# A decoder layer with a mixture of experts: another order of each engine's work within an expert, other PSUM banks for the last two chunks, and the experts' output tiles evicted by ScalarE

## The reference, cut to what matters

```python
def _mlp(h, wg, wu, wd):
    return jax.nn.silu(h @ wg) * (h @ wu) @ wd
C = int(np.ceil(1.25 * N * 2 / 16))          # 640 rows for each expert, N = 4096
expert_inputs = jnp.zeros((E, C, d)).at[idx_flat, pos_c].add(x_pair)   # gathered tokens
expert_outputs = jax.vmap(_mlp)(expert_inputs, w_gate, w_up, w_down)   # F = 704
output_tokens = (expert_outputs[idx_flat, pos_c] * (vals_flat * within)[:, None])...
return x + _mlp(x, sw_gate, sw_up, sw_down) + output_tokens
```

## Time and profile before

| what | value |
|---|---|
| median of 3 runs | 1927.52 us (1926.8 to 1929.26) |
| profiled execution, its own time | 1925.47 us |
| its span, first to last instruction | 1923.8 us |
| TensorE busy (matmuls) | 1810.9 us, 94% |
| VectorE, ScalarE, GpSimd busy | 1243.3, 889.0, 1054.0 us |
| mean granted TensorE clock | 0.971 |

### The profile page before, as it was taken

How to read it: one execution, slowest core, us unless ns; L and a number is a source line. 1 busy time by engine, 2 the same in 40 slices (tenths; PEclk the granted TensorE clock), 3 DMA queues, 4 the chain that set the end, 5 groups by cost and what they waited for, 6 DMA issues and landing times.

```text
span 1923.8 us, 27307 instructions
## 1 busy us (share of the span) xinstructions
PE 1810.9 (94%) x9689; PEld 1595.2 (83%) x9689; DVE 1243.3 (65%) x2579; ACT 889.0 (46%) x1638; POOL 1054.0 (55%) x809
## 2 busy tenths in 40 slices
PE   9999999999999999999998998899889988998897
PEld 6888888888878888888888888888788888888887
DVE  6677777778644444437675777567666766686663
ACT  5465556564643333315454445344534553554341
POOL 3444546556442222246657755775577557755861
PEclk9999999999999999999999999999999999999999
DMA  9354555443423332245547555654575456546642
GB/s 330 117 143 130 133 144 148 147 140 103 116 37 44 45 78 45 44 101 132 103 133 165 122 100 140 156 125 101 135 160 118 106 142 151 114 115 146 145 86 28
DMA packets 236007, 229.35 MB, mean 119 GB/s; under 512 B 169664, under 2 KB 169920, under 8 KB 234592
## 3 DMA queue, kind: packets, MB, share of 16 engines
q1 hardware_dynamic: 210432, 174.50, 33.4%
q0 software_dynamic: 25440, 53.11, 15.7%
HBM read 138.80 MB, written 49.97 MB: 98 GB/s over the span
## 4 chain that ended last, share of the span: by engine, by line
PE 50%; DVE 16%; POOL 14%; issue 9%; ACT 6%; DMA 4%; POOLq 0%; SPq 0%; DVEq 0%; ACTq 0%
PE ps L73 31%; PE ps L2111 8%; PE ps L2140 7%; POOL out_tokens L1570 6%; POOL buffer L1528 5%; ACT buffer L1618 4%; PE ps L1003 3%; DMA buffer<-in_wts 3%; DVE buffer L1804 2%; DVE ps L1855 2%; POOL buffer L1533 1%; DVE buffer L1812 1%; DVE buffer L1936 1%; ACT buffer L1670 1%; PE ps L1147 1%
## 5 line engine op out<-in xcount | busy, mean ns | idle before, releaser
L73 PE MATMUL ps<-buffer,buffer 128*128 128x512 f32 (+1 forms) x4596 | 912.1, 357 | 33.1 <-DVE buffer L1913 32.4
L73 PEld LDWEIGHTS ps<-buffer,buffer 128*128 128x128 f32 x4596 | 785.9, 188 | 143.6 <-DVE buffer L1913 36.6
L1618 ACT ACTIVATE buffer<-buffer 128x512 fp32r<-128x512 f32 (+7 forms) x555 | 379.5, 736 | 245.2 <-DMA buffer<-in_wts 148.3
L2140 PE MATMUL ps<-buffer,buffer 128*128 128x512 f32 (+1 forms) x1921 | 439.1, 389 | 3.1 <-DVE buffer L1848 3.1
L2140 PEld LDWEIGHTS ps<-buffer,buffer 128*128 128x128 f32 x1921 | 357.9, 188 | 77.1 <-issue 3.7
L2111 PE MATMUL ps<-buffer,buffer 128*128 128x320 f32 x2016 | 341.6, 333 | 64.5 <-ACT buffer L1618 63.3
L2111 PEld LDWEIGHTS ps<-buffer,buffer 128*128 128x128 f32 x2016 | 332.4, 209 | 69.8 <-ACT buffer L1618 67.3
L1528 POOL TENSOR_TENSOR buffer<-buffer,buffer 128x512 fp32r<-128x512 f32 x176 | 260.3, 1729 | 26.2 <-ACT buffer L1618 26.2
L1533 POOL TENSOR_TENSOR buffer<-buffer,buffer 128x768 fp32r<-128x768 f32 x48 | 89.6, 1866 | 237.8 <-ACT buffer L1618 237.3
L521 POOL DMA_INDIRECT slots<-pairs,slot_u x64 | 63.5, 992 | 209.1 <-DVE slot_u L990 192.0
L1570 POOL DMA_INDIRECT out_tokens<-buffer,slot_list x79 | 130.0, 1645 | 55.7 <-DVE buffer L1936 32.5
(11 more groups left out here) (162 smaller groups left out, 1865.8 us busy)
## 6 DMA issues: line engine op xcount, KB each, us to landing
buffer<-in_wts SPq DMA_DIRECT2D x128, 512.0 KB, 3.7
buffer<-in_wts SPq DMA_DIRECT2D x33, 256.0 KB, 3.5
buffer<-in_xT SPq DMA_DIRECT2D x8, 1024.0 KB, 5.5
buffer<-in_ctxT SPq DMA_DIRECT2D x8, 1024.0 KB, 8.0
out_tokens<-buffer SPq DMA_DIRECT2D x8, 1024.0 KB, 4.3
tokens_normed<-buffer SPq DMA_DIRECT2D x32, 256.0 KB, 2.9
out_tokens<-buffer POOLq DMA_DIRECT2D x32, 256.0 KB, 6.7
buffer<-in_x SPq DMA_DIRECT2D x7, 1024.0 KB, 5.7
```

The lines of the kernel that those rows point to most:

```text
L73: last = pe.matmul(out, left, right, start=(c == 0 and i == 0), stop=(c == len(parts) - 1 and i == 2))
L1618: return act.activation(dst, src, ACT.Copy)
L2140: ins = pe.matmul(down_bank[(n + i) % 2][:, part_cols], left, right, start=(c == 0 and k == 0), stop=(c == FC - 1 and k == len(passes) - 1))
```

## The change

No instruction's work is changed in the attention blocks or the shared expert; the order of some of SyncE's loads and transposes for expert 0 is. In the expert loop:

1. The order of each engine's calls is written out anew, in whole blocks, and the counts that its waits use come from lists of names in that order (`numbered`) in place of formulas. `pair_high` is cut into `block_high` and `sum_high`, `pair_low` into `block_low` and `sum_low`, the second add of `third` becomes `up_b`, and each x_top, x_hi, x_sum_hi, gather, turn, scatter and evict can stand by itself. TensorE's own order stays the same.
2. The units of chunk 4 (half A) and chunk 5 (half A) take the two down banks; paired chunks 1 and 3 always take `even_banks`, chunk 2 `odd_banks`; 0A even, 0B and 4B odd, 5B the bank ps[1]. The product is written over the gate's bank in place of a third one. Waits follow (`bank_free`).
3. The experts' output tiles are evicted by ScalarE, as a copy with the routing weight as scale, in place of VectorE's multiplication.
4. `third_sum` has two buffers that take turns; some buffers move in SBUF to make room.

The core of the diff:

```diff
-    banks = [(ps[0], ps[1], ps[2]), (ps[3], ps[6], ps[7])]
+    even_banks, odd_banks = (ps[0], ps[1], ps[2]), (ps[3], ps[6], ps[7])
+    pair_banks = {1: even_banks, 2: odd_banks, 3: even_banks}
...
+    def plain_banks(e, c, j):
+
+        a = tiles_before[B + e] % 2
+        if c == FC - 1:
+            return [(down_bank[1 - a], down_bank[1 - a]), (ps[1], ps[1])][j]
+        if (c, j) == (4, 0):
+            return down_bank[a], down_bank[1 - a]
+        return (even_banks, odd_banks)[j][0:2]
...
+            elif what == "m36":
+                low_ready(pe, e, 1, 0)
...
+            elif what == "4A":
+                pe.wait_ge(s_ost, tiles_before[B + e])
+            elif what == "4B":
+                pair_silu_ready(pe, e, "a", 2)
+                low_ready(pe, e, 2, 0)
+            elif what == "5A":
+                product_ready(pe, e, 4, 0)
+            elif what == "5B":
+                low_ready(pe, e, 3, 0)
...
+        def evict(e, t):
+            g = B + e
+            n = tiles_before[g] + t
+            act.wait_ge(s_add[t], 16 * adds_of(g, t))
...
+            gate = slot_list[:, e * ET + t, 1:2]
+            for i, cols in enumerate(column_parts(g, t)):
+                act.wait_ge(s_down, n + i + 1)
+                act.activation(ost[:, t, cols], down_bank[(n + i) % 2][:, cols], ACT.Copy, scale=gate).then_inc(s_ost, 1)
```

More of the change, by code:

```diff
@@ L1269, in phase2, with numbered @@
[L1269 to L1281, removed]
+    def numbered(first, steady):
+        number = {}
+        for name in first.split():
+            number[name, 0] = len(number) + 1
+        for e in range(E):
+            for name in steady.split():
+                of = e + name.endswith("+")
+                if of < E:
+                    number[name.rstrip("+"), of] = len(number) + 1
+        return number
@@ L1283, in pair_no, with pair_before @@
     def pair_no(e, c):
         return NP * e + PAIRED.index(c)
[L1286 to L1290, removed]
+    def pair_before(e, c, k):
+        n = pair_no(e, c) - k
+        return n // NP, PAIRED[n % NP]
+    def plain_banks(e, c, j):
[5 more added lines that the diff above has]
+        return (even_banks, odd_banks)[j][0:2]
@@ L1300, in product_count @@
[L1300 to L1308, removed]
     FIRST = WC - 1
@@ L1583, in gpsimd @@
                 pool.wait_ge(s_list, 16)
-                gather(0)
+                for t in range(ET):
+                    gather(0, t)
             for c in range(FC):
@@ L1757, in scalar @@
             plain_hi(e, 0, 1)
-            for i in range(8, NPL):
-                plain_high(e, i)
+            plain_high(e, 10)
             paired_silu_a(e, 1)
@@ L1789, in scalar @@
             if more:
-                tokens(e + 1)
-                pair_high(e + 1, 2)
-                for i in range(2, 5):
-                    plain_high(e + 1, i)
+                x_top(e + 1, 0)
+                x_top(e + 1, 1)
+                sum_high(e + 1, 2)
+                x_top(e + 1, 2)
+            evict(e, 0)
+            if more:
+                plain_high(e + 1, 2)
+                plain_high(e + 1, 3)
+                x_top(e + 1, 3)
+                x_top(e + 1, 4)
+                x_hi(e + 1, 0)
+            evict(e, 1)
+            if more:
+                x_hi(e + 1, 1)
+                plain_high(e + 1, 4)
+            evict(e, 2)
+            if more:
+                x_sum_hi(e + 1, 0)
+                x_sum_hi(e + 1, 2)
+                x_sum_hi(e + 1, 1)
+                x_sum_hi(e + 1, 3)
+            evict(e, 3)
+            evict(e, 4)
     def vector(dve):
@@ L1915, in evict @@
         def evict(g, t):
-            job, part, _, _ = groups[g]
             n = tiles_before[g] + t
@@ L2006, in vector @@
             paired_product(e, 1, 0)
+            if more:
+                pair_sums(e + 1, 0)
+            paired_lo(e, 1, 0)
+            third(e, 2)
             paired_product(e, 1, 1)
-            paired_lo(e, 1, 0)
+            up_b(e, 2)
+            second(e, 3)
             paired_lo(e, 1, 1)
-            third(e, 2)
-            second(e, 3)
             up_a(e, 2)
@@ L2123, in down @@
                     pe.wait_ge(s_ost, n - 1)
+                if g >= B and t < 2:
+                    bank_free(g - B, f"d{t}")
                 cols = slice(t * P, (t + 1) * P)
```

633 lines of the change are left out of this document (357 added, 276 removed).

## The result

The changed kernel takes 1881.53 us in the median of 4 runs (1878.29 to 1884.4), against 1927.52: a ratio of 0.976, 95% interval 0.9743 to 0.9777. That is 46 us less, where 124 were forecast, and it lies outside the range of 1786 to 1855. The profiled execution's span is 1876.5 us.

What follows compares the result with a forecast made beforehand. TensorE, busy 94%, was taken as the bound, so only its idle time and clock could give. Expert 0 ends at 943.95; 14 x 56.5 = 791.0 and 65.6 lead to 1800.6; plus 1.7 and 2.0: 1804 us, range 1786 to 1855.

Steps and rivals of the forecast that it cites:

- The long wait and its clock: In each expert, ahead of product 2.2: the 4.26 us wait and the 2.88 us of slow clock both go.
- Weight sums ahead of 1A's low part: Ahead of product 3.6: VectorE's sums make TensorE wait 0.8 us, plus 0.2 for the queue, 1.0 for each expert.
- Wait in 4B: 4B no longer needs 3A's low part, so 1.99 us goes; 5B's bank was to be early by 1.7 us.
- rival A: GpSimd's scatters held beside VectorE's token splits; 3.6 us wait ahead of product 3.6, not 0.8; 1843 us, chance 0.13.
- Rival C: TensorE's clock falls all the same after 1 us idles, costing 2.9 us each expert; 1847 us, chance 0.05.
- Evictions: Five for each expert on ScalarE, 0.65 us each: cost 0 in the down product, with 1.3 to 1.6 us cover.
- Expert 0: Shared down's tile 2 waits 1.5 us, first units 1.8 more; it ends at 943.95 against 943.77, nothing won.
- The end: The last stretch, 72.92 us, loses its wait (3.98), clock (2.9) and 0.4: 65.6 us, to 1800.6.
- the hand schedule: TensorE's parts of one expert laid out at full clock, 55.5 us, plus 1.0 of waiting: 56.5 for each expert.

Runs made afterwards that it cites:

- The one move in the kernel before: Kernel before, with ScalarE making the high part of chunk 3's next block ahead of 5A's silu, its sums' ahead of the tokens' copies: 1906.94 us, 0.989.
- the runs above: The best kernel with 4B's second bank waiting for 3A's low part, 1832.81 us; the changed kernel with weight sums moved ahead of chunk 3's adds, 1864.92 us.
- products in PSUM: Changed kernel with the B halves' silu and product written into the gate's PSUM bank: 1814.89 us, 0.9415.
- the two edits: Changed kernel with B halves' silu and product in PSUM, and all gathers ahead of the low parts of blocks 0 and 1: 1800.17 us, 0.9338.
- one bank dependence: 4B's second bank again waits for the low part of 3A: 1937.63 us in the changed kernel, 1832.81 us in the best kernel.
- the evictions' place: Experts' evictions back on VectorE among the token work: 1887.49 us in the changed kernel, 1813.78 us in the best kernel.
- the bank wait in the best kernel: The best kernel with 4B's second bank waiting for the low part of 3A again: 1832.81 us, 0.952.
- the best kernel: Changed kernel with both B halves' products in PSUM and all gathers ahead of the low parts of blocks 0 and 1: 1800.17 us, 0.9338.

## Why the prediction was wrong

**The long wait and its clock: right.** GpSimd's scatters start 4.8 us before an expert ends (1068.21 against 1073.00), where 5.3 were forecast; load 8 goes out at 7.4 of the next expert (5.5 forecast), `first` of chunk 2 ends at 12.9 and TensorE needs it at 15.8. The one move in the kernel before confirms the chain.

**The step that failed first: "Weight sums ahead of 1A's low part", 1.0 us for an expert.** It measured 2.5 and 1.6 of clock behind it, 3.1 of the 5.0 us that an expert took too long. The four sums took 4.3 us, from 16.0 to 20.4; the prediction had the start right to the tenth and bounded them by 3.4, with the longest duration of the row of before (2.26), where VectorE met one GpSimd subtraction. Here it met two in a row and was held over both. The bound was not one. Load 1 went out at 12.4, not 10.5, so its 2 us of slack were gone too, but VectorE's waits for it are 0.3 us at most.

**The second step that failed: "Wait in 4B", put at nothing.** The 1.99 goes, but 1.4 came back ahead of 5B, and 0.5 in down. The prediction took the 3.7 us from product 3.3 to the low part of 3A from the trace of before. It was 6.7 here (1044.62 to 1051.28), because VectorE's whole queue was late by the 4.35 us low part of 1B, by a sum of 2.10 and by a product of 2.27, all held. The prediction set the two queues side by side only at the sums and, in rival A, at the scatters, and did not ask what else would now run at once. Counted by cause, that missing term is the larger error: with the low part and product of the B halves no longer held, the period is 57.15, near the 56.5 forecast, since GpSimd then also meets the sums a microsecond earlier and the clock stays whole.

**Clock.** The prediction gave the wait ahead of 3.6 no clock, because 1.8 us of idle had left it whole. The kernel before spoke for that more strongly than the earlier trace rows show: of its 15 waits of 1.8 to 2.5 us in 4B, 14 left it at 1.00. In the changed kernel all 14 waits of 2.3 to 2.7 us ahead of 3.6 were followed by half clock. So the length of an idle does not settle it, here or in the runs above where 1.9 us lowered it and 2.65 did not; what does is open. Rival C named this effect, for idles of 1 us in each expert; the idles of 1.2 to 1.5 us here and with products in PSUM left the clock whole.

**Evictions: near right.** They take 0.69 us (0.65 forecast), eviction 0 ends at 49.4 after down's start at 41.7: tile 2 begins at 50.0. Down waits for no eviction, with 0.5 us to spare where 1.6 were forecast. Their worth was put at nothing and is 14 us once nothing else binds.

**Expert 0.** Forecast to start at 885.65 and end at 943.95; it was 888.02 and 949.95. Down waited 2.55 for the eviction where 1.5 was forecast, and half clock lay behind it. **The end:** 65.0 against 65.6.

By the prediction's sum: 6.0 for expert 0, 14 x 5.0 = 70.6 for the periods and -0.6 for the end lead from 1800.6 to 1876.6; the span is 1876.5. Where VectorE is not held on TensorE's chains, the whole work takes 1800 us. That is near the 1804 forecast in part by luck: its periods are 55.67 where 56.5 were forecast, 12 us less, and its expert 0 ends 9.5 us later than forecast. The periods still say that the hand schedule was right for a VectorE that GpSimd does not stop.

**The rule that was on the table.** The trace: in the places read here, two-buffer operations of VectorE end when GpSimd's run of subtractions ends, 3.2 us in place of 0.4, 4.4 and 7.7 in place of 0.5; those that read PSUM and one buffer kept 0.48 beside them. The Trainium skill says it in SBUF — State Buffer, SBUF: two separate sides: the shared pair of ports is an exclusive lock for a whole instruction, also between a VectorE operation with two SBUF inputs and a GpSimd operation that reads SBUF. The trace agrees and goes further, since one VectorE operation was held over four GpSimd instructions. The kernel before showed holds too, at the low parts of the token sums, 1.9 us in the median in place of 0.82. Rival A named the rule, and put it at the scatters in place of the sums and products. That section of the Trainium skill tells of starved descriptor writing for another mode of VectorE's operations, its two-port mode, so that A's use of it went beyond what is written there; here the first three scatters, beside VectorE's two-buffer operations, took 1.9 to 2.6 us in place of 1.55, and no wait of TensorE stands on them.

## What to carry to other kernels

Before moving an operation, list for its new place which VectorE operations with two SBUF inputs and which GpSimd operations will run side by side, and give each of the first the length of the whole run of the second as its upper bound. Where such an operation stands in a chain that TensorE waits for, keep one of its inputs in PSUM, or put DMA issues rather than subtractions beside it: the two edits took 81 us off the changed kernel. A busy time that rises while work is taken away is the sign to look for, and a part's worth depends on the others: one bank dependence cost 56 or 33 us, the evictions' place 6, hardly measurable, or 14.

## What the runs showed of the hardware that was not expected

- A VectorE operation of 0.48 us was held for 7.68, through four GpSimd subtractions that followed each other without a gap, and had been issued 0.6 us ahead of the first of them, at the end of a gather. GpSimd's gathers alone did not hold it: four sums at 0.42 to 0.43 us beside two gathers.
- Not every meeting lasts a whole run. In the kernel before, three low parts of the token sums took 4.93 us (0.82 each alone) beside three subtractions that took 5.55 (1.3 each alone, in the changed kernel): the two engines went in turn, and each held the other. Nothing waited for them there. What decides between turns and a whole run is not shown.

```profile
1331.88 4.93 DVE L1840 TENSOR_TENSOR buffer<-buffer,buffer 128x640 fp32r<-128x640 f32 x3
```

- ScalarE's silu in place in a PSUM bank, and VectorE's product over it, are no slower than from and to SBUF: 0.42 us for 0.44, and 0.49 for 0.48.
- The same idle of TensorE can lower its clock or leave it. Waits of 2.45 us in 4B left it at 1.00 in expert 0 of the kernel before; with the one move in that kernel, waits of 2.45 us at the same place brought 1.2 GHz in 11 of 15 experts, and 1.9 us did so in 4 of 14 with the bank wait in the best kernel.
